# A hand-written slot schedule: other distances between the steps of each chunk, on one core

## The reference, cut to what matters

```python
x = x + tanh(g_xattn[0]) * xattn0(layernorm(x), ctx, group_prob, mask0)   # 16 heads of 8, scores + mask, softmax, * group_prob, @ v, @ wo
x = x + tanh(g_ffn[0])   * moe0(layernorm(x))    # top 2 of 8 experts; tokens scattered to slots of their expert (capacity), gelu, gathered, weighted
x = x + tanh(g_xattn[1]) * xattn1(layernorm(x), ctx, mask1)               # the same without group_prob, one mask for all
x = x + tanh(g_ffn[1])   * moe1(layernorm(x))    # all 8 experts for every token, weighted by the top two gates
```

## Time and profile before

| | us |
|---|---|
| three timed runs: median, lowest, highest | 1041.09, 1038.82, 1042.5 |
| the profiled execution: its own time | 1043.33 |
| its span | 1041.5 |
| PE busy, DVE, ACT, POOL | 785.9, 630.6, 609.2, 613.5 |
| granted TensorE clock, mean | 0.894 |

### The profile page before, as it was taken

The page is one execution under the profiler, slowest core; times in us unless marked ns, Lnnn a source line. Parts: engine busy times, 40 slices in busy tenths (PEclk is TensorE's granted clock), DMA queues, the critical chain, the costliest instruction groups (busy, mean ns, idle before and its releaser), DMA issues.

```text
span 1041.5 us, 20382 instructions
## 1 busy us (share of the span) xinstructions
PE 785.9 (75%) x6552; PEld 629.0 (60%) x6552; DVE 630.6 (61%) x1832; ACT 609.2 (58%) x2578; POOL 613.5 (59%) x978
## 2 busy tenths in 40 slices
PE   2279988788942799992117878676888789999997
PEld 1157766566731699992005556555666577888885
DVE  0268997796961222220146877877888857666664
ACT  1378997686930444440127777877999745444442
POOL 7456667787777100000687778776632387777775
PEclk9688998898985799997568888999999999999998
DMA  6869734564532122225134356336520000000000
GB/s 169 219 144 296 166 104 105 119 141 119 119 124 118 55 67 72 73 63 160 38 89 110 97 117 163 108 69 138 130 72 12 22 20 21 21 21 21 12 11 21
DMA packets 80066, 97.53 MB, mean 94 GB/s; under 512 B 7952, under 2 KB 67285, under 8 KB 79000
## 3 DMA queue, kind: packets, MB, share of 16 engines
q1 hardware_dynamic: 75864, 87.99, 32.7%
q0 software_dynamic: 4096, 8.25, 3.1%
HBM read 59.18 MB, written 41.58 MB: 97 GB/s over the span
## 4 chain that ended last, share of the span: by engine, by line
PE 29%; issue 24%; POOL 16%; ACT 13%; DVE 11%; DMA 7%; SPq 0%; POOLq 0%; ACTq 0%; DVEq 0%
ACT exp L641 9%; PE psum L558 4%; PE psum L560 4%; PE psum L559 4%; DMA got_rows<-scratch_y,slot_get 4%; DVE shift L804 3%; PE psum L408 3%; POOL got_rows L1209 3%; PE psum L396 2%; POOL xn_rows L1129 2%; POOL q_operand L1276 2%; POOL scratch_xe L1191 2%; PE psum L376 2%; PE psum L421 2%; PE psum L399 2%
## 5 line engine op out<-in xcount | busy, mean ns | idle before, releaser
L641 ACT ACTIVATE exp<-psum,shift 128x120 f32<-128x120 f32 x1024 | 364.6, 437 | 119.4 <-DVE shift L804 119.1
L641 ACT ACTIVATION_READ_ACCUMULATOR exp<-psum,shift 128x1 f32 x1024 | 272.4, 281 | 0.0
L804 DVE TENSOR_REDUCE shift<-psum 128x4 f32<-128x480 f32 x256 | 165.9, 648 | 91.6 <-PE psum L399 89.4
L408 PE MATMUL psum<-ident,exp 128*120 128x128 f32 x1024 | 166.5, 288 | 17.5 <-DVE exp_T L816 9.9
L396 PE MATMUL psum<-neg_rows,const_bf 128*128 128x480 bf16 x256 | 101.9, 398 | 79.8 <-issue 37.3
L1276 POOL TENSOR_TENSOR q_operand<-q_operand 128x512 f32<-128x512 f32 x96 | 126.0, 1312 | 55.4 <-DVE q_operand L1050 50.2
L1050 DVE SCALAR_TENSOR_TENSOR q_operand<-psum,comb,q_operand 128x256 f32<-128x256 f32 x256 | 111.6, 479 | 70.5 <-ACT q_operand L754 70.3
L754 ACT ACTIVATE q_operand<-psum 128x512 f32<-128x512 f32 x128 | 76.4, 599 | 112.8 <-PE psum L560 112.7
L408 PEld LDWEIGHTS psum<-ident,exp 128*120 128x120 f32 x1024 | 124.8, 145 | 27.9 <-DVE exp_T L816 12.5
L558 PE MATMUL psum<-w_T_high,xn_T_high 128*128 128x512 f32 x256 | 106.8, 417 | 4.8 <-DVE w_T_low L1016 4.3
L399 PE MATMUL psum<-k_operand,q_operand 128*128 128x240 bf16 x512 | 101.3, 282 | 0.0
(11 more groups left out here) (139 smaller groups left out, 1708.7 us busy)
## 6 DMA issues: line engine op xcount, KB each, us to landing
q_operand<-scratch_q SPq DMA_DIRECT2D x32, 384.0 KB, 6.5
k_operand<-scratch_k SPq DMA_DIRECT2D x32, 360.0 KB, 9.3
scratch_q<-parts SPq DMA_DIRECT2D x16, 384.0 KB
scratch_k<-parts SPq DMA_DIRECT2D x16, 360.0 KB
scratch_q<-parts SPq DMA_DIRECT2D x16, 256.0 KB
scratch_xe<-in_zero_rows SPq DMA_DIRECT2D x8, 512.0 KB, 10.3
scratch_k<-parts SPq DMA_DIRECT2D x16, 240.0 KB
xe_rows<-scratch_xe SPq DMA_DIRECT2D x16, 192.0 KB, 2.5
```

Of the source, the lines that this page charges most:

```text
L408: ins = pe.transpose(ps[0:S2, T_BANKS[G % 2], u * S:(u + 1) * S], atts[l].expS[:, G % RING_E, u, :], ident[:, :])
L641: ins = act.activation(atts[l].expS[:, G % RING_E, u, :], ps[:, S_BANKS[G % 3], u * S2:(u + 1) * S2], ACT.Exp, bias=atts[l].shift[:, i % 2 ...
L804: dve.tensor_reduce(atts[l].shift[:, i % 2, 4 * r:4 * r + 4], ps[:, S_BANKS[G % 3], 0:4 * S2].rearrange("p (h k) -> p h k", h=4), AX_X, AL ...
```

## The change

It moves table entries and a few fixed slot numbers; no computation is added or removed.

```diff
-LAG_TURN, LAG_INV, LAG_ROWS, LAG_SUM, LAG_O = 3, 6, 8, 9, 10
+LAG_TURN, LAG_INV, LAG_ROWS, LAG_SUM, LAG_O = 3, 6, 8, 9, 11
...
 FAR = dict(k_project=0, k_take=1, k_part0=2, k_left0=3, k_part1=3, k_left1=4, k_out=(5, 7, 9), k_fetch=16,
-           stat=0, power=2, norm=5, turn=10, turned=11, bias=10,
-           q_project=14, q_take=15, q_part0=16, q_left0=17, q_part1=17, q_left1=18, q_out=(19, 21, 23), q_fetch=26)
+           stat=0, power=1, norm=4, turn=12, turned=13, bias=14,
+           q_project=16, q_take=17, q_part0=18, q_left0=19, q_part1=19, q_left1=20, q_out=(21, 23, 25), q_fetch=28)
...
-POST = dict(stat=0, power=2, norm=5, turn=10, turned=11, gate=14, logits=15, top=16, one_hot=17, exp=18,
-            ranks=21, take_ranks=22, positions=23, slots=24, send=26, weigh=22, add_bo=23)
+POST = dict(stat=0, power=1, norm=4, turn=12, turned=13, gate=16, logits=17, top=18, one_hot=19, exp=20,
+            ranks=23, take_ranks=24, positions=25, slots=27, send=28, weigh=24, add_bo=29)
+
+TIGHT = dict(stat=0, power=1, norm=4, turn=7, turned=8, gate=11, logits=12, top=12, one_hot=13, exp=14,
+             ranks=16, take_ranks=17, positions=17, slots=18, send=19, weigh=17, add_bo=20)
+
+def post_at(j):
+    return POST if j < 5 else TIGHT
...
-OUT = dict(project=1, add=2)
+OUT = dict(project=2, add=4)
...
-SLOTS_ALL = after_slot(NCH - 1) + POST["send"] + CB * TOPK + 1
+SLOTS_ALL = after_slot(NCH - 1) + TIGHT["send"] + CB * TOPK + 1
...
 # GpSimd, behind(l, s)
-                if l == 1 and 2 < P < NCH and -16 <= o < -8:
-                    bring(CB * P + (o + 16) // 2, o % 2)
+                ahead = 16 if P == 3 else 22
+                if l == 1 and 2 < P < NCH and 0 <= o + ahead < TOPK * CB:
+                    bring(CB * P + (o + ahead) // 2, o % 2)
...
-            if l == 0 and s % 16 == 12 and s // 16 + 1 < NCH:
+            if l == 0 and s % 16 == 2 and s // 16 + 1 < NCH:
                 masks(s // 16 + 1)
...
 # GpSimd, attention(l)
-                if r == 1 and i < B:
-                    spread_v(l, i)
+                if r == 0 and 0 <= i - 1 < B:
+                    spread_v(l, i - 1)
...
 # SyncE, behind(l, s)
             if l == 0 and s // 16 + 1 < NCH:
-                if s % 16 == 8:
-                    load_masks(s // 16 + 1)
+                if s == 0:
+                    load_masks(1)
+                if s % 16 == 6 and s // 16 + 2 < NCH:
+                    load_masks(s // 16 + 2)
```

More of the change, by code:

```diff
@@ L467, in behind @@
                     out_project(l, j)
-                if o == POST["turn"]:
+                if o == post_at(j)["turn"]:
                     turn_rows(1, n)
-                if o == POST["gate"]:
+                if o == post_at(j)["gate"]:
                     gate_logits(n)
-                if o == POST["ranks"] and l == 0:
+                if o == post_at(j)["ranks"] and l == 0:
                     ranks(n)
@@ L668, in early @@
             for j in range(NCH):
-                if s - after_slot(j) == POST["turned"]:
+                if s - after_slot(j) == post_at(j)["turned"]:
                     take_turned(1, l * NCH + j)
@@ L680, in behind @@
                 o, n = s - after_slot(j), l * NCH + j
-                if l == 0 and o == POST["exp"]:
+                if l == 0 and o == post_at(j)["exp"]:
                     on.wait_ge(rt, step_count(n, 7))
                     act.activation(gate_e[:, 1, :], gate_e[:, 0, :], ACT.Exp).then_inc(r_exp, 1)
-                if l == 1 and o == POST["exp"]:
+                if l == 1 and o == post_at(j)["exp"]:
                     on.wait_ge(rt, step_count(n, 8))
@@ L928, in early @@
                     add_out(l, c)
-                if s - after_slot(c) == POST["logits"]:
+                if s - after_slot(c) == post_at(c)["logits"]:
                     take_logits(l * NCH + c)
-                if l == 0 and s - after_slot(c) == POST["take_ranks"]:
+                if l == 0 and s - after_slot(c) == post_at(c)["take_ranks"]:
                     take_ranks(c)
@@ L944, in behind @@
                 o, n = s - after_slot(j), l * NCH + j
-                if o == POST["stat"]:
+                if o == post_at(j)["stat"]:
                     stat_rows(1, n, l, j)
-                if o == POST["top"]:
+                if o == post_at(j)["top"]:
                     top_two(n)
-                if o == POST["one_hot"]:
+                if o == post_at(j)["one_hot"]:
                     one_hot(n)
@@ L955, in behind @@
                 if l == 0:
-                    if o == POST["positions"]:
+                    if o == post_at(j)["positions"]:
                         positions(n)
                 else:
-                    if o == POST["weigh"]:
+                    if o == post_at(j)["weigh"]:
                         combination(j)
@@ L1244, in behind @@
                 o = s - after_slot(j)
-                if o == POST["power"]:
+                if o == post_at(j)["power"]:
                     powers(1, l * NCH + j)
-                if o == POST["norm"]:
+                if o == post_at(j)["norm"]:
                     normalise_rows(1, l * NCH + j, j)
-                if l == 0 and o == POST["slots"]:
+                if l == 0 and o == post_at(j)["slots"]:
                     slots(j)
-                if l == 1 and o == POST["add_bo"]:
+                if l == 1 and o == post_at(j)["add_bo"]:
                     add_bo(j)
-                if l == 0 and 0 <= o - POST["send"] < CB * TOPK:
-                    send(j, o - POST["send"])
+                if l == 0 and 0 <= o - post_at(j)["send"] < CB * TOPK:
+                    send(j, o - post_at(j)["send"])
         def attention(l):
@@ L1409, in behind @@
             for c in range(NCH):
-                if l == 1 and s - after_slot(c) == POST["turned"] + 1:
+                if l == 1 and s - after_slot(c) == post_at(c)["turned"] + 1:
                     send_xT(c)
```

## The result

The changed kernel takes 1109.43 us, the median of four runs (1104.62 to 1112.67), against 1039.95 us of the kernel before in four runs beside it: a ratio of 1.0669, 95% interval 1.0615 to 1.0723. It is 69 us slower where 13 us less were forecast, and lies outside the range of 1005 to 1047.

A forecast was written before the change was run, and what follows sets the result against it. PE and POOL hold each other up; without these stalls a chunk costs what its busiest engine needs, plus bank waits. Terms sum to -13.3 us: 1043.3 to 1030.0, by the median 1028 us; range 1005 to 1047, the forecast's own 1018 to 1039.

The forecast's parts named there:

- Together 4.0 us a chunk: Shared-bank waits in slots 12, 0 and 9 of a chunk: 2.4, 1.1 and 0.5 us; bounds nothing and 7.6.
- 0.5 left over: Steady chunks: time beyond ACT's work and the 4.0 us of bank waits, put at 0.5 us a chunk.
- Chunks 3 to 5: -9.2: Layer 0, chunks 3 to 5: 95 us, from ACT's 81.45 + 13.5, against 104.2, so 9.2 us less.
- POOL sets the pace, 34.2 each: Layer 1, chunks 2 to 4: POOL bounds them at 34.2 us each; chunks 1 to 4 take 138 against 153.0.
- The first rival: The shared banks cost nothing: chunks 3 to 5 of layer 0 take 88 us, the kernel 1007 us; chance 0.27.
- +3.7: Start of layer 0: `powers` of chunk 2 and chunk 1's masks delay chunk 1's q and normalising, 3.7 us more.
- +3.5: Layer 0, chunk 1: chunk 2's q is projected two slots later, 3.5 us more, at best 1, at worst 6.
- -4.5: Tail of layer 0: POOL through chunk 5's scatters 2.2 us earlier, 2.41 us landing wait covered, 4.5 us less.
- Behind the attention of layer 1: 0: Expert phases and change-over, so also what follows layer 1's attention: untouched by the change, 0 us.
- The bubbles fall at the lower clock: Slots 12, 0, 9 of chunks 2 to 6, both layers: products cost double, 3.6 us more a chunk; 1064 us, chance 0.10.
- the last sign of being wrong: A clock that stays low in the dense chunks would show the forecast wrong.

The follow-up runs named there:

- run 1: Changed kernel with four calls of the two shared PSUM banks moved (k projection, both turned rows, gate), none waiting for an emptying under two slots back: 1043.7 us, ratio 1.0044.
- r_both: Kernel before with masks, rows and gathers earlier, plus bank clashes put into slots 0 and 12: 1076.59 us, ratio 1.0276.
- run 3: Changed kernel with the power two slots behind the statistics again, as before the change: 1115.18 us, ratio 1.0728.
- clean_again: The kernel of run 1 repeated unchanged on the second chip: 1066.27 us, ratio to before 1.0211.
- clean_p2: The kernel of run 1 with chunk 2 prepared by the old table in both layers, second chip: 1049.23 us, ratio 1.0069.
- tail_p2_again: The kernel of clean_p2 with wide distances for all chunks in layer 1, second chip: 1043.37 us, ratio 1.0004.
- runs 1 to 4: Changed kernel with four bank calls moved, k projection alone moved, or power later; kernel before with slot 0's clash added: ratios 1.0044, 1.0418, 1.0728, 1.023.

## Why the prediction was wrong

**The mechanism was right, its size was not.** The step that failed is the term "Together 4.0 us a chunk" of the two shared banks. The places, the releaser and the bank wait that was the model for it all came as written; the time lost is 7.0 and 8.1 us a chunk in layer 0, 4.5 and 6.0 in layer 1 (run 1). Four things were left out. The clock: with it the text itself came to 7.6, and that was put aside as a rival with a chance of 0.10, though the row it rested on, a product of 1.97 us, stood at the lower clock. (In that row the bank wait of 0.71 us was not what had lowered it: the turned rows at 574.16 took 1.09 us already, behind 5.16 us of waiting for POOL.) The gate, which may wait for DVE in the same slot. The second bubble, behind the weighted sums. And the sum over places: r_both indicates that clashes in slots 12 and 0 are not independent. How the 8.1 us divide among these is not shown.

A second term failed beside it, the "0.5 left over" in "ACT's work + 4.0 + 0.5". In run 1, without clashes, what is left over ACT's busy time is (91.5 - 79.5) / 3 = 4.0 us a chunk in chunks 3 to 5 of layer 0 and (142.9 - 113.8) / 4 = 7.3 in chunks 1 to 4 of layer 1. A chunk does not shrink to what its busiest engine needs when one stall is taken away.

**The relief was real**, but its steps were mixed with the bubbles. "Chunks 3 to 5: -9.2": without clashes it is -12.7 (run 1); with them +11.5. "POOL sets the pace, 34.2 each" in layer 1 was wrong: with clashes the chunks take 37 to 43 us, and POOL waits for DVE. Without them chunks 1 to 4 take 142.9 us, where the sum had 138 (with 34.2 a chunk although POOL's need was put at 34.4). The first rival's 88 us for chunks 3 to 5 of layer 0 lay below POOL's own 91.7; no run came under 91.5.

**Start.** "+3.7" and "+3.5" were near: the first maximum of chunk 2 came 10.4 us later against 7.2. PE waits 10.37 us for the k operand of chunk 1 and 4.46 for the q operand of chunk 2; run 3 gives the power's share (4.4 us at chunk 1), the pair clean_again and clean_p2 that of chunk 2's whole table.

**Tail of layer 0.** "-4.5" was wrong. The last scatter is issued at 380.59, 48.7 us behind the last maximum; before it was 340.99, 46.8 behind. The 2.41 us of the earlier trace rows are gone, but routing of the last chunk starts three slots later, through scaling and projection, and POOL normalises its rows 27.4 us behind the last maximum, where it was 20.8; the step had not carried the three slots on to POOL. The next stage gained 0.6 us.

**Behind the attention of layer 1: 0** was wrong by 8. The short distances hold there too, though no scatter is urgent, and a slot of the expert phase is fuller for POOL; taking them away gave 5.9 us back (clean_p2 and tail_p2_again).

**The rivals.** "The bubbles fall at the lower clock" came nearest, at 1064: the waits and the clock are as it says, and the last sign of being wrong came too (chunk 2 of layer 0 at a clock of 0.91, before 1.00). It is still 45 us short. Of these, by the table and with that rival's 3.6 us for each of its chunks, 10 are in chunks 3 to 5 of layer 0 (115.7 - 95 - 10.8) and 12 in chunks 1 to 4 of layer 1 (161.0 - 138 - 10.8), where a relief had been counted that did not come with the clashes in place; 8 lie behind layer 1, the rest at the starts, in chunks 6 and 7 and in the tail. What would happen to DVE's gather waits was right in kind: 42.3 us before, 23.9 after. Two pages of the Trainium skill spoke against this change, and the trace agrees with both in direction. The Trainium skill (Perfetto Trace Analysis, Identifying Performance Opportunities) says that the same gap repeating on the engine that should be saturated can mean that there is too little PSUM for the next tile; here 58 us of PE waits stand before the same three calls. The Trainium skill (TensorE: Matmul & The Clock Gate, A second HAM failure mode: psum-queue depth-cycling) describes short idle times of PE, from cycling through PSUM banks, behind which the clock swings; here the clock of chunks 3 to 5 of layer 0 is 0.85, before 0.92 and in run 1 0.99.

## What to carry to other kernels

When work is moved in a table of slots, walk every ring that the moved steps share, and write down for each call how many slots of the pacing engine lie between it and the emptying it waits for: with two or more run 1 has only short waits for these banks (the longest 1.7 us), with none such a place cost about 2 us a chunk, and two of them 5. A wait for a buffer that runs an engine's lead out was paid three times here: the wait, the slower clock of what follows, and the next hand-over behind it; take the row with the low clock as the price, not half of it. A long wait of an engine that is early need not be a loss (POOL's 73.6 us in run 1). A relief counts where its wait comes last: the masks alone brought nearly all of it in layer 0, while in layer 1 the rows brought little until the gathers came earlier too.

## What the runs showed of the hardware

That the granted clock falls behind the bank waits was in the second rival; that two places add more than their sum, at a lower clock than either alone, was not. Unexpected is the difference between chips. On the second one PE halts inside the weighted sums of layer 0, mostly in slots 12 and 13 of chunks 3 to 6, while the profile names nothing that it waits for. In clean_again:

```profile
201.51 0.32 PE L429 MATMUL psum<-exp_T,v_spread 120*32 120x128 f32 x2 [1.14 <-issue]
202.98 0.31 PE L429 MATMUL psum<-exp_T,v_spread 120*32 120x128 f32 x2 [1.15 <-issue]
204.42 0.39 PE L429 MATMUL psum<-exp_T,v_spread 120*32 120x128 f32 x1 [1.13 <-issue]
```

The 32 products, 1.08 us elsewhere, stretch to over 5. The twelve profiles of the second chip have 1 to 10 us of such halts in the sums, the four of the first none, the same kernel (run 1) included. In that stretch DMA is busy at a share of 0.93 (192 to 206 us), in run 1 on the first chip at 0.71 (186 to 198). Whether PE's instructions come late there was not tried. The halts are at most 10 us, while the ratio of run 1's kernel differs by 1.7% between the chips, some 17 us, so the rest of that difference is open. It is why the ratios of runs 1 to 4 and the later ones are not compared to better than about 2%.
